# A graph network kernel: half-array products grouped behind the transposes of a block, bias and edge weights at 128 rows

## The chip, the cores and the metric

The kernel runs on one core of a Trainium2 chip. The metric is device microseconds of one execution, the median of several runs. One more execution was taken with the hardware profiler; its instructions are what the views below show. TensorE is called PE in them (PEld its weight load), VectorE DVE, ScalarE ACT, GpSimd POOL, SyncE SP; SPq is what SP issues to its DMA queue.

## The reference

50,000 nodes with 64 features, 50,000 edges sorted by destination. Four residual layers follow each other, each on `h = relu(layernorm(x))`:

```python
# 0: gated edges
m = sigmoid([h[dst], h[src], attr] @ W_f + b_f) * softplus(... @ W_s + b_s) * exp(-dist**2/18)
x = x + h + segment_sum(m, dst)
# 1: plain edges, one edge weight e
x = x + segment_sum(relu([h[src], h[dst], e] @ W1 + b1) @ W2 + b2, dst)
# 2: two attention layers (GATv2, 5 heads, self loops), softmax over dst, mean of heads, relu
x = x + g @ Wfc + bfc
# 3: graph convolution with degrees, batch norm, elu
x = x + layer3(h)
```

## The kernel before, in words

Edges and nodes are cut into 392 tiles of 128, four tiles a block, 98 blocks a stage (`blocks`, L724: six blocks, then a loop unrolled four times). Stages follow each other: setup, a node pass, `gated_edges` (PE 325 to 1055 us), a node pass, `plain_edges` (1243 to 1958), a node pass, `attention_logits` (2176 to 2910), softmax, messages, `attention_nodes` (3398 to 3650), the logits of the second attention layer (3708 to 4437), messages, `attention_nodes` again with the last layer (4925 to 5225), a node pass, `copied_edges`, the finish. Engines run their own instruction streams and meet at semaphores; the order of the work on each engine is written out by hand in its `body`.

Three of the stages gather rows of both ends of an edge with `NearRows`. SP loads for block n (L874 to L885) the edge positions `relb` (L877), four windows of node rows `near` (L882) and the rows that lie outside them, `rest` (L884), into `z`; it waits for `z_used` of block n-4 first. POOL gathers the source rows with four indirect DMAs (L870), also after `z_used` of block n-4. DVE makes the one-hot `hotT` (L894). PE then takes, in `turn` (L897), for two tiles at a time two fp32 transposes of `z` into the bank `zTp` (L905, full array) and eight matrix instructions, four products, of `near` with `hotT` (L909); the latter write 64 partitions each, two of them side by side on half of the array, and add to what the transposes wrote. The last one posts `z_used`. Another engine copies `zTp` to `zT`.

- `gated_edges`: PE does `turn(n)` with two transposes of the edge attributes (L1016), `scatter(n-2)` (L767), `project(n)`, which begins with a bf16 product of three ones rows and `bias3` (L1027; the bias is cut into three bf16 parts), followed by L1030 and L1034. ACT copies zT (L1057).
- `plain_edges`: PE does `turn(n)`, `second(n-1)` (L1219), `degrees(n-1)` (L1226), `scatter(n-2)`, `first_layer(n)`: a two-row fp32 product of the edge weights `aux` (L1239) and two half-array products (L1241). ACT copies zT (L1269), makes the one-hot of the scatter and the relu `uT` (L1274). SP stores the messages (L1189) five loads behind.
- `attention_logits`: PE does `turn(n)`, `project_whole(n-1)` (L1611, six groups of two fp32 products of 256 columns), `contract(n-2)` (L1594 to L1599, 32-column strips, posts `alp_ready`), `project_halves(n-1)` (L1618, 64-row tiles). DVE copies zT (L1681) and takes the logits (L1674); the copy of block n-1 comes behind the wait for `alp_ready` of block n-3.
- `attention_nodes`, second pass (g = 1): PE does two transposes (L2064), two more (L2080), `project` (L2073, 64-row tiles), and `last_layer`: a product of one row of ones and `bfc`, 256 columns in fp32 (L2086), then L2089. DVE multiplies (L2179), adds (L2184) and writes the new x (L2190); POOL adds (L2149 to L2158); ACT L2118, L2128.

In setup a chain of dependent DVE instructions prepares the weights; L485 to L492 cut the bias of `gated_edges` into three bf16 parts on three partitions, 128 columns wide.

## Time and profile before

| | us |
|---|---|
| median of three runs | 6153.05 |
| their range | 6148.98 to 6160.13 |
| profiled execution, first to last instruction | 6214.2 |

| engine | busy us | share |
|---|---|---|
| PE | 4419.2 | 71% |
| PE weight load | 3124.8 | 50% |
| DVE | 3312.8 | 53% |
| ACT | 3117.1 | 50% |
| POOL | 3300.7 | 53% |

The profiled execution has no time of its own beside its span; it is 1.0% above the median of the others. Busy shares are an average over some fifteen stages with different limits, so the slices of single stages have to be read. Matmuls overlap in the array and their ends are modelled: the distance from start to start tells the pace. A row of a stretch gives its start and end, its length, busy us and instructions of PE, PE weight load, DVE, ACT and POOL, then the granted TensorE clock, the busy share of the DMA engines and GB/s. An idle time in brackets behind an instruction is that of its engine just before it, with what ended it. The granted TensorE clock, 1.00 for 2.4 GHz, is a mean of 0.845 over the span.

### The profile page before, as it was taken

Reading aid. Unit: us, or ns where it says so; the run is one execution under the profiler, and the core shown is the slowest. Engines: PE = TensorE matmul, PEld = TensorE weight load, DVE = VectorE, ACT = ScalarE, POOL = GpSimd, SP = SyncE. Lnnn points to the kernel's source line nnn. Section 1 sums busy time; section 2 is a strip of 40 time slices with the busy share of each in tenths; the row PEclk is TensorE's granted clock in tenths of the full one; section 3 lists DMA queues with packets and bytes.
Section 4 is the critical chain, followed back from the end, with each engine's and each line's share of the span. In section 5 each row is a group of like instructions: output and inputs, shape, how many; then the busy total and the mean of one; then the engine's idle time right before and its main releaser. Section 6 shows DMA issues by size and latency. Waiting matters only on the chain. (4 is left out here: it accounts for less than half of the span.)

```text
span 6214.2 us, 127051 instructions
## 1 busy us (share of the span) xinstructions
PE 4419.2 (71%) x31655; PEld 3124.8 (50%) x31655; DVE 3312.8 (53%) x7235; ACT 3117.1 (50%) x8158; POOL 3300.7 (53%) x3372
## 2 busy tenths in 40 slices
PE   0078898089896089997498749999669896055564
PEld 0056676066664056665376326666447663054452
DVE  3833333766666432233787963333488788611156
ACT  0267776644555434444386214444358524644447
POOL 0855553155552165553586975555268687666620
PEclk6589998599998599999699979999879998576775
DMA  7545554655554744444133644444323333622224
GB/s 187 169 118 122 123 123 98 176 106 106 109 110 106 241 105 112 113 113 101 33 83 76 153 124 109 113 112 114 83 48 83 77 88 84 138 45 45 44 58 130
DMA packets 1393493, 665.08 MB, mean 107 GB/s; under 512 B 835537, under 2 KB 1341325, under 8 KB 1391594
## 3 DMA queue, kind: packets, MB, share of 16 engines
q1 hardware_dynamic: 1307980, 580.76, 37.4%
q0 software_dynamic: 64256, 65.93, 5.9%
q10 hardware_dynamic: 21124, 17.02, 0.9%
q8 instruction: 35, 0.57, 0.0%
q14 instruction: 98, 0.80, 0.0%
HBM read 393.69 MB, written 269.08 MB: 107 GB/s over the span
## 5 line engine op out<-in xcount | busy, mean ns | idle before, releaser
L870 POOL DMA_INDIRECT z_e<-h_d,src_i x784 | 756.8, 965 | 652.8 <-PE zTp_e L909 453.0
L1656 ACT ACTIVATE leak_l<-tp_l,bcat 128x512 f32<-128x512 f32 x588 | 365.9, 686 | 665.1 <-issue 422.4
L1681 DVE COPY zT_l<-zTp_l 128x512 f32<-128x512 f32 x196 | 135.5, 691 | 1005.7 <-DMA near_d<-gout_a 341.3
L754 ACT ACTIVATE hot_e<-iota_n,rel 128x256 f32<-128x256 f32 x1176 | 501.0, 502 | 322.9 <-DMA hn_a<-g_d 247.2
L784 DVE TENSOR_TENSOR acc<-acc,part_e 128x128 f32 x1176 | 336.8, 286 | 610.1 <-DMA hn_a<-g_d 247.4
L767 PE MATMUL part_e<-z_e,hot_e 128*128 128x128 f32 x1568 | 313.4, 376 | 436.7 <-DVE acc L784 226.9
L870 POOL DMA_INDIRECT z_l<-h_d,src_i x392 | 389.6, 994 | 326.4 <-PE zTp_l L909 229.2
L870 POOL DMA_INDIRECT z_l<-g_d,src_i x392 | 387.9, 989 | 324.9 <-PE zTp_l L909 230.0
L767 PEld LDWEIGHTS part_e<-z_e,hot_e 128*128 128x128 f32 x1568 | 285.2, 279 | 465.0 <-DVE acc L784 240.4
L905 PE MATMUL zTp_e<-ident,z_e 128*128 128x128 f32 x784 | 175.8, 306 | 480.4 <-DMA z_e<-rest_d 472.8
L1351 POOL DMA_INDIRECT z_e<-h_d,src_i x392 | 370.8, 946 | 222.7 <-issue 104.8
L767 PE MATMUL part_e<-m_e,hot_e 128*128 128x128 f32 x3136 | 408.5, 286 | 61.2 <-issue 28.1
L1661 ACT ACTIVATE leak_l<-tp_l,bcat 128x256 f32<-128x256 f32 x784 | 307.8, 475 | 283.1 <-PE tp_l L1618 252.2
L767 PEld LDWEIGHTS part_e<-m_e,hot_e 128*128 128x128 f32 x3136 | 392.5, 200 | 78.4 <-issue 39.9
L767 PEld LDWEIGHTS part_m<-m_m,hot_m 128*128 128x128 f32 x3136 | 365.9, 192 | 88.0 <-DVE acc L784 80.2
L767 PE MATMUL part_m<-m_m,hot_m 128*128 128x128 f32 x3136 | 403.2, 282 | 2.4 <-DVE acc L784 1.1
L1611 PE MATMUL tp_l<-zT_l,wcat 128*128 128x256 f32 x1176 | 376.2, 402 | 22.6 <-DVE zT_l L1681 14.1
L754 ACT ACTIVATE hot_m<-iota_n,rel 128x256 f32<-128x256 f32 x784 | 334.3, 497 | 110.0 <-PE part_m L767 108.5
L905 PEld LDWEIGHTS zTp_e<-ident,z_e 128*128 128x128 f32 x784 | 80.4, 143 | 566.5 <-issue 554.6
L905 PE MATMUL zTp_l<-ident,z_l 128*128 128x128 f32 x784 | 174.1, 304 | 264.8 <-DMA z_l<-rest_d 244.8
L1611 PE MATMUL tp_l<-zT_l,wswap_l 128*128 128x256 f32 x1176 | 355.6, 384 | 1.2 <-issue 1.2
L2179 DVE TENSOR_TENSOR prod_a<-xl_a,wself_a 128x640 f32<-128x640 f32 x392 | 303.9, 815 | 41.7 <-PE xl_a L2073 37.3
(362 smaller groups left out, 11787.7 us busy)
## 6 DMA issues: line engine op xcount, KB each, us to landing
near_e<-near_d SPq DMA_DIRECT2D x784, 64.0 KB
near_l<-near_d SPq DMA_DIRECT2D x784, 64.0 KB
h_d<-h SPq DMA_DIRECT2D x84, 448.0 KB
near_d<-h SPq DMA_DIRECT2D x84, 448.0 KB
m_d<-m_m SPq DMA_DIRECT2D x196, 138.0 KB
relb_e<-rel_d SPq DMA_DIRECT2D x196, 128.0 KB
z_e<-rest_d SPq DMA_DIRECT2D x196, 128.0 KB
relb_l<-rel_d SPq DMA_DIRECT2D x196, 128.0 KB
```

Source lines behind the costliest of these rows:

```text
L754: ins = self.nc.scalar.activation(self.hots[k][:, t, :], self.S["iota_n"][:, :], ACT.Abs, scale=-1.0, bias=self.S["rel"][:, ds(n * BLK + t ...
L767: mm = self.nc.tensor.matmul(self.parts[t // 2][:, t % 2, w, :], self.hots[k][:, t, w * P:(w + 1) * P], m[:, t, :], start=True, stop=True)
L784: ins = self.nc.vector.tensor_tensor(x, x, part[:, t % 2, :, 0:x.shape[2]], ALU.add)
L870: self.nc.gpsimd.indirect_dma_start(out=self.z[n % RINGS][:, t, SIDES[t % 2]], out_offset=None, in_=self.table[:, :], in_offset=bass.Indir ...
L905: self.nc.tensor.matmul(zTp[:, t * P:(t + 1) * P], self.z[k][:, t, :], ident[:, :], start=(t == 0), stop=False, is_transpose=True, skip_gr ...
L1351: nc.gpsimd.indirect_dma_start(out=z[k][:, t, 0:C], out_offset=None, in_=S["h_d"][:, :], in_offset=bass.IndirectOffsetOnAxis(ap=S["src_i"] ...
L1611: mm = nc.tensor.matmul(by_side(tp[q])[:, side], left[:, q, :], by_side(zT[k])[:, side], start=True, stop=True)
L1656: nc.scalar.activation(leak[u % 2][:, q, :], tp[q][:, :], ACT.Relu, bias=bcat[:, 0, q:q + 1], scale=1.0 - SLOPE).then_inc(leak_ready, 1)
L1661: nc.scalar.activation(by_side(leak[u % 2][:, 3 + q, :])[:, side], tp[3 + side][:, q * 2 * P:(q + 1) * 2 * P].rearrange("p (r e) -> p r e" ...
L1681: nc.vector.tensor_copy(zT[k][:, :], zTp[k][:, :]).then_inc(zT_ready, 1)
L2179: nc.vector.tensor_tensor(prod[k][:, 2 * q:2 * q + 2, :].rearrange("p t (h c) -> p t h c", h=H), xl[slot(u, q)][:, :, 0:HC].rearrange("p t ...
```

## The change

`turn` keeps its four transposes alone and no longer waits for `hotT`; the eight near products move to `spread`, which waits for `hotT`, goes over the windows outside and the tiles inside, and posts `z_used`. In `gated_edges` `spread(n)` stands behind the attribute transposes, in `attention_logits` behind `project_whole(n-1)`. In `plain_edges` the first layer is divided into `weights` (the edge weight product) and the rest, both a block later, as are the second layer, the degrees, the scatter and their helpers on ACT and DVE; the tail is a block longer. `aux`, `w1t`, `bias3` and `ones3` have 128 partitions of zeros beyond their rows; `bfc` is cut into three bf16 parts, `bfc3`, and the last layer adds it as one bf16 product with 128 rows.

```diff
--- before.py
+++ after.py
@@ -166,11 +166,12 @@
         w0 = sb("w0", [P, 2 * C])
         w0s = sb("w0s", [P, 2 * C])
         w0a = sb("w0a", [P, 2 * C])
-        bias3 = sb("bias3", [3, BLK * C], BF16)
-        ones3 = sb("ones3", [3, P], BF16)
+        bias3 = sb("bias3", [P, BLK * C], BF16)
+        bfc3 = sb("bfc3", [P, BLK * C], BF16)
+        ones3 = sb("ones3", [P, P], BF16)
         w1 = sb("w1", [P, C])
         w1s = sb("w1s", [P, C])
-        w1t = sb("w1t", [2, P])
+        w1t = sb("w1t", [P, P])
         b1 = sb("b1", [P, 1])
         w1b = sb("w1b", [P, P])
         b1b = sb("b1b", [P, C])
@@ -408,6 +409,8 @@
                 chain(nc.vector.memset(S["wfc"][:, :], 0.0))
                 chain(nc.vector.memset(S["w1b"][:, :], 0.0))
                 chain(nc.vector.memset(S["w1t"][:, :], 0.0))
+                chain(nc.vector.memset(S["bias3"][:, :], 0.0))
+                chain(nc.vector.memset(S["bfc3"][:, :], 0.0))
                 chain(nc.vector.memset(S["ones3"][:, :], 1.0))
                 nc.vector.memset(ones[:, :], 1.0).then_inc(s_blank, 1)
                 dve.wait_ge(s_loaded, 15 * 16)
@@ -489,7 +492,17 @@
                 for i in range(1, 3):
                     chain(nc.vector.scalar_tensor_tensor(out=whole[:, :], in0=cut[:, i, :], scalar=ident[0:3, i:i + 1], in1=whole[:, :],
                                                          op0=ALU.mult, op1=ALU.add))
-                chain(nc.vector.tensor_copy(S["bias3"][:, :].rearrange("p (q c) -> p q c", q=2), wide(whole[:, :], 1, 2)))
+                chain(nc.vector.tensor_copy(S["bias3"][0:3, :].rearrange("p (q c) -> p q c", q=2), wide(whole[:, :], 1, 2)))
+
+                for i in range(3):
+                    chain(nc.vector.tensor_copy(cut_b[:, 0:C], S["bfc"][0:3, :]))
+                    chain(nc.vector.tensor_copy(cut[:, i, 0:C], cut_b[:, 0:C]))
+                    chain(nc.vector.tensor_tensor(S["bfc"][0:3, :], S["bfc"][0:3, :], cut[:, i, 0:C], ALU.subtract))
+                chain(nc.vector.tensor_scalar(whole[:, 0:C], cut[:, 0, 0:C], ident[0:3, 0:1], None, ALU.mult))
+                for i in range(1, 3):
+                    chain(nc.vector.scalar_tensor_tensor(out=whole[:, 0:C], in0=cut[:, i, 0:C], scalar=ident[0:3, i:i + 1], in1=whole[:, 0:C],
+                                                         op0=ALU.mult, op1=ALU.add))
+                chain(nc.vector.tensor_copy(S["bfc3"][0:3, :].rearrange("p (q c) -> p q c", q=BLK), wide(whole[:, 0:C], 1, BLK)))
 
                 chain(nc.vector.tensor_reduce(bl_one[:, :], bl_col[:, :], AX.X, ALU.add))
                 chain(nc.vector.scalar_tensor_tensor(out=S["gcol"][:, :], in0=bl_one[:, :], scalar=1.0 / H, in1=S["gcol"][:, :],
@@ -899,15 +912,18 @@
         k, ident = u % RINGS, self.S["ident"]
         pe.wait_ge(gathered[k], 16 * BLK * (i + u // RINGS + 1))
         self.arrived(pe, u, i)
+        for t in range(BLK):
+            self.nc.tensor.matmul(zTp[:, t * P:(t + 1) * P], self.z[k][:, t, :], ident[:, :], start=(t == 0), stop=False, is_transpose=True, skip_group_check=True)
+
+    def spread(self, pe, n, u, zTp):
+
+        k = u % RINGS
         pe.wait_ge(self.hotT_ready, n + 1)
-        for r in range(0, BLK, 2):
-            for t in (r, r + 1):
-                self.nc.tensor.matmul(zTp[:, t * P:(t + 1) * P], self.z[k][:, t, :], ident[:, :], start=(t == 0), stop=False, is_transpose=True, skip_group_check=True)
-            for w in range(WIN):
-                for t in (r, r + 1):
-                    cols = slice(t * P, (t + 1) * P)
-                    mm = self.nc.tensor.matmul(zTp[SIDES[1 - t % 2], cols], self.near[k][:, t, w, :], self.hotT[u % 2][:, w, cols], start=False,
-                                               stop=(w == WIN - 1), skip_group_check=True)
+        for w in range(WIN):
+            for t in range(BLK):
+                cols = slice(t * P, (t + 1) * P)
+                mm = self.nc.tensor.matmul(zTp[SIDES[1 - t % 2], cols], self.near[k][:, t, w, :], self.hotT[u % 2][:, w, cols], start=False,
+                                           stop=(w == WIN - 1), skip_group_check=True)
         mm.then_inc(self.z_used, 1)
 
 
@@ -1015,6 +1031,7 @@
                     for q in range(2):
                         tr = nc.tensor.transpose(aTp[:, q * P:(q + 1) * P], att[k][:, 2 * q:2 * q + 2, :].rearrange("p t c -> p (t c)"), ident[:, :])
                     tr.then_inc(att_used, 1)
+                    near.spread(pe, n, u, zTp)
 
                 def project(n, u):
                     k = u % 2
@@ -1147,7 +1164,7 @@
         def ps(n, shape, count=2):
             return [ctx.enter_context(nc.psum_tensor(f"{n}_{name}_{k}", shape, F32)) for k in range(count)]
 
-        z, m, aux = ring("z", [P, BLK, 2 * C]), ring("m", [P, BLK, MOVED]), ring("aux", [2, 2, P])
+        z, m, aux = ring("z", [P, BLK, 2 * C]), ring("m", [P, BLK, MOVED]), ring("aux", [P, 2, P])
         zT, uT = ring("zT", [P, BLK * P], 2), ring("uT", [P, 2 * P], 2)
         zTp, uTp, mp, count = ps("zTp", [P, BLK * P]), ps("uTp", [P, 2 * P]), ps("mp", [P, BLK, C], 1)[0], ps("count", [P, TILES], 1)[0]
         sums = NodeSums(nc, S, ctx, name, WIDTH, S["deg_in"])
@@ -1175,13 +1192,13 @@
                     k = u % RINGS
                     near.load(sp, n, u)
                     need(sp, u_ready, n - RINGS + 1)
-                    sp.dma_start(aux[k][:, :, :], ew_rows[ds(n, 1)].rearrange("n r h e -> (n h) r e")).then_inc(aux_in[k], 32)
+                    sp.dma_start(aux[k][0:2, :, :], ew_rows[ds(n, 1)].rearrange("n r h e -> (n h) r e")).then_inc(aux_in[k], 32)
 
                 def load_last(n, u):
                     k, r0 = u % RINGS, n * BLK * P
                     near.load(sp, n, u)
                     sp.wait_ge(u_ready, n - RINGS + 1)
-                    sp.dma_start(aux[k][:, 0, :], io["edge_weight1"][r0:r0 + 2 * P, :].rearrange("(h e) a -> h (e a)", h=2)).then_inc(aux_in[k], 16)
+                    sp.dma_start(aux[k][0:2, 0, :], io["edge_weight1"][r0:r0 + 2 * P, :].rearrange("(h e) a -> h (e a)", h=2)).then_inc(aux_in[k], 16)
                     sp.dma_start(aux[k][0:1, 1, 0:LAST_E - 2 * P], ew[:, r0 + 2 * P:E]).then_inc(aux_in[k], 16)
 
                 def store(n, u):
@@ -1231,12 +1248,14 @@
                     pe.wait_ge(m_ready, n + 1)
                     sums.multiply(pe, n, u % 2, m[u % RINGS])
 
-                def first_layer(n, u, i):
+                def weights(n, u, r):
                     k = u % RINGS
-                    pe.wait_ge(aux_in[k], 32 * (i + u // RINGS + 1))
-                    pe.wait_ge(zT_ready, n + 1)
+                    pe.wait_ge(aux_in[k], 32 * (r + 1))
                     need(pe, uT_ready, n - 1)
                     nc.tensor.matmul(uTp[u % 2][:, :], S["w1t"][:, :], aux[k][:, :, :].rearrange("h r e -> h (r e)"), start=True, stop=False, skip_group_check=True)
+
+                def first_layer(n, u):
+                    pe.wait_ge(zT_ready, n + 1)
                     for half in range(2):
                         mm = nc.tensor.matmul(uTp[u % 2][half * C:(half + 1) * C, :], S[("w1", "w1s")[half]][:, :],
                                               zT[u % 2][:, :].rearrange("p (r h e) -> p h r e", h=2, e=P)[:, half],
@@ -1246,14 +1265,23 @@
                 def body(n, u, i):
                     turn(n, u, i)
                     if has(n, 1):
-                        second(n - 1, u + 1)
-                        degrees(n - 1, u + 1)
+                        weights(n - 1, u + UN - 1, i + (u - 1) // RINGS)
+                    near.spread(pe, n, u, zTp[u % 2])
+                    if has(n, 1):
+                        first_layer(n - 1, u + 1)
                     if has(n, 2):
-                        scatter(n - 2, u + UN - 2)
-                    first_layer(n, u, i)
+                        second(n - 2, u)
+                        degrees(n - 2, u)
+                    if has(n, 3):
+                        scatter(n - 3, u + UN - 3)
                 blocks(pe, body)
-                second(NB - 1, NB - 1)
-                degrees(NB - 1, NB - 1)
+                weights(NB - 1, NB - 1, (NB - 1) // RINGS)
+                first_layer(NB - 1, 1)
+                second(NB - 2, 0)
+                degrees(NB - 2, 0)
+                scatter(NB - 3, NB - 3)
+                second(NB - 1, 1)
+                degrees(NB - 1, 1)
                 for n in range(NB - 2, NB):
                     scatter(n, n)
                 pe.wait_ge(s_zero, 1)
@@ -1262,18 +1290,24 @@
 
             @block.scalar
             def _(act):
+                def hidden(n, k):
+                    act.wait_ge(u_ready, n + 1)
+                    need(act, mp_ready, n - 1)
+                    nc.scalar.activation(uT[k][:, :], uTp[k][:, :], ACT.Relu, bias=S["b1"][:, 0:1]).then_inc(uT_ready, 1)
+
                 def body(n, u, i):
                     k = u % 2
                     act.wait_ge(z_used, n + 1)
                     need(act, u_ready, n - 1)
                     nc.scalar.copy(zT[k][:, :], zTp[k][:, :]).then_inc(zT_ready, 1)
                     if has(n, 1):
-                        sums.hot(act, n - 1, 1 - k)
-                    act.wait_ge(u_ready, n + 1)
-                    need(act, mp_ready, n - 1)
-                    nc.scalar.activation(uT[k][:, :], uTp[k][:, :], ACT.Relu, bias=S["b1"][:, 0:1]).then_inc(uT_ready, 1)
+                        hidden(n - 1, 1 - k)
+                    if has(n, 2):
+                        sums.hot(act, n - 2, k)
                 blocks(act, body)
-                sums.hot(act, NB - 1, 1)
+                hidden(NB - 1, 1)
+                for n in range(NB - 2, NB):
+                    sums.hot(act, n, n % 2)
 
             @block.vector
             def _(dve):
@@ -1311,14 +1345,18 @@
 
                 def body(n, u, i):
                     near.hot(dve, n, u, i)
-                    los = sums.windows(dve, n - 3) if has(n, 3) else None
-                    digits(n, u)
-                    if has(n, 3):
-                        sums.add(dve, n - 3, los)
+                    los = sums.windows(dve, n - 4) if has(n, 4) else None
                     if has(n, 1):
-                        message(n - 1, u + UN - 1, i + (u - 1) // RINGS)
+                        digits(n - 1, u + 1)
+                    if has(n, 4):
+                        sums.add(dve, n - 4, los)
+                    if has(n, 2):
+                        message(n - 2, u + UN - 2, i + (u - 2) // RINGS)
                 blocks(dve, body)
-                message(NB - 1, NB - 1, (NB - 1) // RINGS)
+                digits(NB - 1, 1)
+                sums.add(dve, NB - 4, sums.windows(dve, NB - 4))
+                for n in range(NB - 2, NB):
+                    message(n, n, n // RINGS)
                 for n in range(NB - 3, NB):
                     sums.add(dve, n, sums.windows(dve, n))
 
@@ -1624,6 +1662,7 @@
                     turn(n, u, i)
                     if has(n, 1):
                         project_whole(n - 1, (u + 1) % 2)
+                    near.spread(pe, n, u, zTp[u % 2])
                     if has(n, 2):
                         contract(n - 2, u % 2)
                     if has(n, 1):
@@ -2083,7 +2122,7 @@
                 def last_layer(n, k):
                     pe.wait_ge(gT_ready, n + 1)
                     need(pe, x_done, n)
-                    nc.tensor.matmul(fcp[:, :, :], S["ones"][0:1, 0:P], wide(S["bfc"][0:1, :], 1, BLK), start=True, stop=False,
+                    nc.tensor.matmul(fcp[:, :, :].rearrange("p t c -> p (t c)"), S["ones3"][:, :], S["bfc3"][:, :], start=True, stop=False,
                                      skip_group_check=True)
                     for q in range(2):
                         mm = nc.tensor.matmul(fcp[:, 2 * q:2 * q + 2, :].rearrange("p t c -> p (t c)"), gT[k][:, q * P:(q + 1) * P], wfc[:, :],
```

## Rows read from the trace of the kernel before

**Rows 1.** Busy time per engine (instruction counts) in slices of gated, plain, logits, second attention_nodes.

```profile
400.00:600.00 200.00, 179.61 (x1510) 139.20 (x1509) 77.47 (x246) 161.97 (x441) 106.13 (x111) 0.96 0.52 122
1400.00:1600.00 200.00, 179.76 (x1360) 127.73 (x1358) 134.97 (x517) 101.12 (x192) 105.17 (x109) 0.95 0.51 107
2330.00:2485.00 155.00, 153.51 (x1224) 100.90 (x1227) 45.94 (x84) 71.70 (x147) 80.39 (x85) 1.00 0.47 112
4971.00:5126.00 155.00, 155.00 (x938) 98.33 (x936) 134.38 (x209) 38.96 (x104) 129.46 (x157) 1.00 0.34 88
```

**Rows 2.** Timeline of TensorE in plain_edges: start us, us, line, idle before and its releaser.

```profile
1509.38 0.43 PE L905 MATMUL zTp_e<-ident,z_e 128*128 128x128 f32 x2 [1.71 <-DMA z_e<-rest_d]
1509.75 0.66 PE L909 MATMUL zTp_e<-hotT_e,near_e 128*64 128x128 f32 x8
1510.34 0.44 PE L905 MATMUL zTp_e<-ident,z_e 128*128 128x128 f32 x2
...
1511.29 0.71 PE L1219 MATMUL mp_e<-w1b,uT_e 128*128 128x128 f32 x4
...
1514.38 0.69 PE L1239 MATMUL uTp_e<-aux_e,w1t 2*128 2x256 f32 x2
1515.00 0.43 PE L1241 MATMUL uTp_e<-zT_e,w 128*64 128x256 f32 x1
```

**Rows 3.** Timeline of SP's DMA queue in plain_edges.

```profile
1507.04 0.72 SPq L884 DMA_DIRECT2D z_e<-rest_d  x1
```

**Rows 4.** Waits in plain_edges, 1400 to 1800: us in total, times, longest us.

```profile
PE zTp_e L905 <- DMA z_e<-rest_d: 27.3, 19, 2.8
...
PE mp_e L1219 <- ACT uT_e L1274: 8.0, 18, 2.2
```

**Rows 5.** Waits in gated_edges, 500 to 900.

```profile
DVE hotT_e L894 <- DMA relb_e<-rel_d: 92.0, 30, 5.7
```

**Rows 6.** Instructions of single lines in plain_edges: count, min/median/max ns.

```profile
L905 PE MATMUL zTp_e<-ident,z_e x218: 272/324/477, 1405.0 to 1800.0; 128*128 128x128 f32 x109
...
L882 SPq DMA_DIRECT2D near_e<-near_d x219: 2/333/727, 1400.0 to 1796.5; - x110
```

**Rows 7.** Waits of SP's queue in the first logits stage, 2330 to 2796.

```profile
SPq L1560 <- DVE zT_l L1681: 3.6, 7, 0.6
```

**Rows 8.** Timeline of TensorE in the first logits stage.

```profile
2500.20 0.38 PE L1599 MATMUL alp_l<-leak_l,alate_l 128*32 128x256 f32 x1
...
2501.57 0.44 PE L905 MATMUL zTp_l<-ident,z_l 128*128 128x128 f32 x2
...
2504.24 0.59 PE L1611 MATMUL tp_l<-zT_l,wswap_l 128*128 128x256 f32 x2
...
2505.11 0.59 PE L1611 MATMUL tp_l<-zT_l,wswap_l 128*128 128x256 f32 x2
```

**Rows 9.** Timeline of VectorE in the first logits stage.

```profile
2502.87 0.69 DVE L1681 COPY zT_l<-zTp_l 128x512 f32<-128x512 f32 x1 [5.04 <-remote]
```

**Rows 10.** Timeline of the second attention_nodes pass, one block.

```profile
5031.99 1.35 PE L2073 MATMUL xl_a<-wl,hT_a 64*128 64x320 f32 x8
...
5032.97 1.55 DVE L2179 TENSOR_TENSOR prod_a<-xl_a,wself_a 128x640 f32<-128x640 f32 x2 [0.36 <-PE xl_a L2073]
...
5033.27 0.69 PE L2086 MATMUL fcp_a<-bfc,ones 1*128 1x256 f32 x2
...
5033.90 0.71 PE L2089 MATMUL fcp_a<-wfc,gT_a 128*128 128x128 f32 x4
...
5034.56 0.69 DVE L2184 TENSOR_TENSOR half_sum_a<-prod_a 128x512 f32<-128x512 f32 x1
...
5035.17 0.42 DVE L2190 TENSOR_TENSOR acc<-fcp_a,xo_a 128x256 f32 x1
```

**Rows 11.** Timeline of VectorE in setup.

```profile
127.89 0.21 DVE L485 CAST cut_b<-b 3x128 bf16<-3x128 f32 x1 [85.48 <-DMA bn<-in_L_gnn_beta_dram]
...
131.70 0.16 DVE L494 TENSOR_REDUCE bl_one<-bl_col 128x1 f32<-128x5 f32 x1
```

## The prediction

> **What bounds the kernel now.** I read the table of stage slices first [rows 1], because the whole-span average mixes stages with different limits. Each of the four edge stages the change touches (gated, plain, logits twice) and the two node passes of attention runs 98 blocks; four gathers on POOL belong to a block, so 200 us with 109 gathers in plain_edges are 27.25 blocks of 7.34 us, gated 7.2 us, logits 155/21.25 = 7.3 us. TensorE (PE) is 99% busy in logits and in the second attention_nodes pass, but only 90% in gated and plain: there about 0.7 us a block is left over, so PE is not what sets their pace.
>
> Next I read the timelines of PE and of SP's DMA queue in plain_edges. PE's block begins with the transposes L905, which waited 1.71 us for the rest rows [rows 2]; SP issued those at 1507.04 and took 0.72 us over it [rows 3], 1.6 us before PE began. The list of SP's own waits is empty in 400 us of either stage: it issues some nine transfers a block, one right behind the other. The waits of the stages say the same: in plain L905 for rest_d [rows 4], in gated hotT for relb, 92 us in 400 [rows 5], both loads from SP's queue. One near-row issue takes 0.33 us at the median and up to 0.73 [rows 6]: four of them a block, so a slow stretch costs SP a microsecond or two. So **SP's queue sets about 7.3 us a block in gated and plain**, whatever PE does. In logits both limits lie together: PE has no gap, and SP waited only 3.6 us in 466, for zT [rows 7], under 0.1 us a block.
>
> **The change, part by part.** The sum is made against the profiled execution's span, 6214.2 us; the median of the unprofiled runs, 6153.05, lies 1.0% below, and I carry the difference in us over to it.
>
> *Transposes together, then products.* Now a block is T2 N8 T2 N8 (matmul records; two near records run side by side). From the first L905 to L909 0.37, then 0.59 to the next L905 [rows 2]: twice 0.96, 1.92 us. A pair of transposes spans 0.43 where one lasts 0.32 [rows 2, 6], so one more costs 0.11; a near pair has the same 128 columns, so 0.11 too. The new order is 0.37 + 2 x 0.11 + 0.59 + 4 x 0.11 = 1.62. PE saves 0.3 us a block, of the two of four switches between full and half array that are gone.
>
> *Padded bias and edge weights.* L1239 with 2 rows takes 0.62 us up to L1241 for two passes of 256 columns [rows 2], where L1611 does four such passes in 0.87 (2504.24 to 2505.11, [rows 8]), 0.43 for two: about 0.2 saved, and perhaps 0.1 where it now stands between full-array work. With the 0.3 that is 0.6 us in plain. L1027 is one bf16 pass, half of that: 0.15, so 0.45 in gated. The copies, memsets and one-hots on ACT and DVE remain as many, only a block later.
>
> What that is worth: in **gated and plain nothing**, since the cover is SP's 7.3 us; PE just waits longer at L905. If that cover were gone, 0.45 x 98 = 44 and 0.6 x 98 = 59 us. Moved steps add no DMA; aux is now released one block later, but relb of block n is issued long after block n-4 was used (gathers of one block start every 7.3 us, four buffers), so the slack of about two blocks loses one. The message is one block later too, and SP stores it five loads behind.
>
> *Logits.* PE's own saving is the 0.3, plus one switch fewer before L1611, less a new one ahead of the near group: 0.3 to 0.4. SP's own work is about 7.2. So 7.3 falls to 7.2 and not to 6.9: I take 0.08 x 196 = **-15** (0 to -78).
>
> *attention_nodes, second pass.* Here PE has no gap and the period is 2.98 us: 938 matmul records in 155 us [rows 1], 18 a block. L2086 begins 5033.27 and L2089 5033.90 [rows 10]: 0.63 us, for two passes of 256 columns from one row and a switch. The new product is one bf16 pass at full array: between 0.12 (the pitch of a 128-column transpose, as a lower end) and 0.31 (half of L1239's 0.62, the upper). PE falls by 0.32 to 0.51, to 2.5 to 2.66. DVE is next: 1.55 + 0.69 + 0.42 = 2.66, with pipelining 2.62, and it sat idle 0.36 for L2073 [rows 10]. So the period goes to 2.62 to 2.66: 0.34 x 98 = **-33** (-31 to -35). That is the firm part.
>
> *Setup.* Thirteen more dependent DVE instructions; their thirteen twins ran 127.89 to 131.70 [rows 11], 3.8 us at 128 columns, these have 64: **+3** (0 to +4), on the path, since DVE's chain ends setup. The two memsets lie beside the loads of the weights; uncovered they would be under 1 us.
>
> *Tail of plain_edges.* One block's first layer, second layer, degrees and scatter more behind the last load: L1219 to L1239 is 3.1 and L1239 to the end of L1241 1.1 [rows 2], so 4.2 at most; part of it lies beside ACT's and DVE's work: **+3** (0 to +4).
>
> Sum: -15 - 33 + 3 + 3 = **-42**; profile 6172, median **6111**.
>
> **The rivals.**
>
> *PE's saving is realized.* SP's pace is not a constant: an issue takes 0.33 to 0.73 us [rows 6], and the unprofiled runs are 61 us shorter than the profiled one; if the long issues are partly the profile's own, the timed runs are closer to PE's pace in gated and plain. For: L1219 also waits for uT [rows 4], which the new order cures. Against: L905 waits for DMA in both stages. Full: -42 - 63 - 44 - 59 = -208, 5945; half of it, more likely, 6028. Chance 0.24.
>
> *A new wait in logits.* L1611 now stands right behind the transposes, and needs zT of the block before. DVE copies that (L1681) after L1599's signal: last L1599 at 2500.20 [rows 8], copy at 2502.87, 0.69 long [rows 9], so zT is there 3.4 us after it. Between the last L1599 and the new place of L1611 lie L1618 (1.37, to 2501.57) and four transposes (0.5): 1.87. PE would stall 1.5 us a block: 6.9 + 1.5 = 8.4 instead of 7.3, x 196 = +216, and with the other terms (-27) 6342. It decides once zT comes more than 1.87 + 0.4 after L1599, so when the copy starts over 1.6 us behind it. Against: the signal is late, as I read it, in the stretch in which issues take 0.7 us instead of 0.3 [rows 6]; that stretch goes with POOL's gather, which starts after the near products, and these come 2.6 us later in the new block (six L1611 groups of 0.43), away from L1599, and with a prompt signal the copy would be done at about 1.1. Chance 0.13. The Trainium skill ("TensorE: Matmul & The Clock Gate", "The cost: per-tile semaphore tail") gives a completion signal a tail of some tens of ns for one increment. By it L1611 never waits and the sum stays at -42. The 2.67 us between L1599 and L1681 don't agree with it, so the wait keeps its chance.
>
> *The bias buys nothing.* If the switch from L2073's 64-row tiles is what costs 0.6 us, the new product pays it too: -5 instead of -33 there, median 6139 to 6150. For: L2089 too follows L2086 only after 0.63, more than two passes take (0.43), so switches are part of the time. Chance 0.12.
>
> *The clock falls in logits*, now at 1.00 [rows 1], to the 0.96 of gated: 4% of 7.2 us is 0.3 a block, +57, median 6168. Chance 0.04. The Trainium skill (same page, "Part 4: PE-mode transpose") says that transposes do not count as TensorE being busy; four in a row would speak for this rival. The present pairs of transposes leave the clock at 1.00, so no run here shows it.
>
> **How the numbers follow.** My forecast 0.47 (6095 to 6130), the rivals 0.24, 0.13, 0.12, 0.04. Faster by more than 0.2% (12 us, about what a measurement of this kernel can tell) is the first two with a little of the third: 0.71; within 0.2%: 0.13; slower: 0.16. The range leaves out the new wait and the last part of PE's full gain: 6000 to 6165.
>
> **What would show it.** After the change: near records x16 in one group behind four transposes, 1.6 us; PE busy in gated and plain down to about 83%, with the gathers per 200 us unchanged (109) and L905 waiting longer for rest_d; logits 155 us slices with PE below 97% and 21.5 blocks; the second attention_nodes pass 2.62 to 2.66 us a block with DVE at 99%. More than 112 gathers in a 200 us slice of plain would prove the pace of SP wrong; idle PE before L1611 with DVE L1681 as releaser would be the new wait.

## The result: 2.1% slower, by a wait in attention_logits that depends on when TensorE's signals come

The change took 6281.02 us (median of 4, 6275.35 to 6288.80) beside 6154.98 us before (6148.98 to 6160.13): ratio 1.0207, 95% interval 1.0194 to 1.0219. The profiled execution spans 6277.4 us, 63 more than that of before. The timed difference is 126; before's profiled execution was 59 us longer than the median of its timed ones, the change's 4 us shorter. The slices of single stages after the change, in the columns of [rows 1]:

```profile
400.00:600.00 200.00, 169.74 (x1573) 146.68 (x1572) 80.03 (x252) 166.33 (x452) 108.98 (x113) 0.97 0.55 126
1400.00:1600.00 200.00, 165.88 (x1406) 132.56 (x1405) 141.00 (x538) 101.95 (x197) 112.82 (x115) 0.97 0.53 112
2330.00:2485.00 155.00, 135.43 (x1123) 93.45 (x1122) 41.07 (x76) 66.51 (x137) 72.79 (x76) 0.99 0.42 102
5050.00:5200.00 150.00, 135.35 (x891) 83.73 (x889) 134.09 (x210) 38.89 (x104) 129.69 (x158) 1.00 0.36 91
```

By POOL's counts gated takes 200/28.25 = 7.08 us a block (7.2 before), plain 6.96 (7.34), logits 155/19 = 8.16 (7.3), the second attention_nodes pass 2.85 (2.98). Such counts are coarse; the lengths of whole stages, from the first to the last matrix instruction, are firmer: gated -23 us, plain -13, the two logits stages +51 and +66, attention_nodes -11. PE, which had no gap in the logits slice of [rows 1], is 87% busy there. So the loss is in logits.

Part of these differences is not the change's. `g3_before_more_sp`, told below, has the old order in all stages and more work on SP in plain_edges alone; its before too took 6154 us, and its profiled execution (6274.8 us) lies near its timed ones (6278). Its slice of gated:

```profile
400.00:600.00 200.00, 186.31 (x1590) 143.96 (x1589) 80.60 (x253) 168.04 (x454) 109.91 (x114) 0.97 0.55 126
```

There gated takes 718.6 us from first to last matrix instruction, as in the change (718.5), where before's profiled execution had 741.4; the two logits stages take 745.2 and 745.9 (752.1 and 749.0 in before), copied_edges, which the change leaves alone, 555.6 (563.2; 555.7 in the change). So in these stages the profiled execution of before was some 40 us longer than another one of the old order, out of the 59. Against `g3_before_more_sp` the change gains nothing in gated and loses 58 and 69 us in logits.

One block of logits in the change, first PE, then DVE:

```profile
2501.96 0.38 PE L1637 MATMUL alp_l<-leak_l,alate_l 128*32 128x256 f32 x1
...
2503.34 0.66 PE L916 MATMUL zTp_l<-ident,z_l 128*128 128x128 f32 x4
2504.88 0.69 PE L1649 MATMUL tp_l<-zT_l,wcat 128*128 128x256 f32 x2 [0.89 <-issue]
...
2507.66 1.09 PE L925 MATMUL zTp_l<-hotT_l,near_l 128*64 128x128 f32 x16
```

```profile
2504.06 0.69 DVE L1720 COPY zT_l<-zTp_l 128x512 f32<-128x512 f32 x1 [5.71 <-issue]
```

L1637 is L1599 of [rows 8], L1649 is L1611, L1720 is L1681. The last product of contract stands at 2501.96; the copy of zT starts 2.10 us later and ends at 2504.75, and project_whole starts at 2504.88, 1.05 us later than its four transposes let it (it follows them after 0.49 us where nothing waits, in `r_after` below). That is the new wait of the second rival, place and all. The list of waits from 2330 to 2796 names DVE for only part of it:

```profile
PE tp_l L1649 <- issue: 33.5, 42, 1.0
PE tp_l L1649 <- DVE zT_l L1720: 17.0, 9, 2.3
```

The starts and ends in the trace settle the rest. In both logits stages together PE sat idle for 202 us ahead of project_whole, against 22 in the kernel before. In 167 of the 196 blocks this idle time was over 0.2 us, and each of these ended 0.05 to 0.15 us behind the end of a copy of zT; before had 12 such blocks. Where PE waited, the last relu of ACT that project_whole could also have waited for had ended 0.9 us or more earlier in nine blocks of ten.

### The profile page after: what moved, and what is told of

Read it like the earlier page. It is cut to its first block and busy times, and to the rows that moved or that the text cites. A ratio compares the mean times of both kernels' runs of the same rounds, so it can differ in the third digit from the quotient of the medians.

```text
span 6277.4 us, 126874 instructions
## 1 busy us (share of the span) xinstructions
PE 4214.5 (67%) x31557; PEld 3136.0 (50%) x31557; DVE 3308.4 (53%) x7250; ACT 3107.8 (50%) x8158; POOL 3294.4 (52%) x3372
## 5 line engine op out<-in xcount | busy, mean ns | idle before, releaser
L1720 DVE COPY zT_l<-zTp_l 128x512 f32<-128x512 f32 x196 | 135.5, 691 | 1130.9 <-issue 300.9
L1649 PE MATMUL tp_l<-zT_l,wcat 128*128 128x256 f32 x1176 | 384.1, 410 | 202.0 <-issue 108.2
L916 PE MATMUL zTp_e<-ident,z_e 128*128 128x128 f32 x784 | 129.7, 289 | 534.6 <-DMA z_e<-rest_d 522.4
L1649 PE MATMUL tp_l<-zT_l,wswap_l 128*128 128x256 f32 x1176 | 366.2, 394 | 0.0
L1649 PEld LDWEIGHTS tp_l<-zT_l,wcat 128*128 128x128 f32 x1176 | 217.1, 198 | 266.9 <-issue 196.8
L1994 DVE TENSOR_TENSOR prod_m<-xl_m,al 128x640 f32<-128x640 f32 x392 | 305.1, 820 | 37.2 <-PE xl_m L1955 14.2
```

What stands on the lines that cost most here:

```text
L916: self.nc.tensor.matmul(zTp[:, t * P:(t + 1) * P], self.z[k][:, t, :], ident[:, :], start=(t == 0), stop=False, is_transpose=True, skip_gr ...
L1649: mm = nc.tensor.matmul(by_side(tp[q])[:, side], left[:, q, :], by_side(zT[k])[:, side], start=True, stop=True)
L1720: nc.vector.tensor_copy(zT[k][:, :], zTp[k][:, :]).then_inc(zT_ready, 1)
L1994: nc.vector.tensor_tensor(heads[:, 2 * q:2 * q + 2], xl[slot(u, q)][:, :, 0:HC].rearrange("p t (h c) -> p t h c", h=H), wide(al[:, ds(n * ...
```

## A condition that none of the two profiles shows alone

The runs of the experiments met the kernel before at two paces: 5835 to 5840 us in five sets and 6154 in a sixth, as in the recorded result. One and the same chip number stands by a set of either pace, so it is a condition that comes and goes, and no fault of one chip (if the number always names the same one). Here are the near-row issues of SP in plain_edges, with the register move ahead of each; this stage is the same in both kernels. First before, as in [rows 6], then the kernel with the last layer's bias alone changed, at the quick pace:

```profile
L882 SPq MOVE near_e<-near_d x218: 3/29/721, 1400.4 to 1796.5; - x109
```

```profile
L895 SPq MOVE near_e<-near_d x258: 29/29/29, 1200.0 to 1597.7; - x129
```

Each of the 258 register moves takes 29 ns at the quick pace; at the slow pace the median is still 29, and the longest took 721. PE's signals follow: at the quick pace, with logits in the old order, DVE's copy starts 0.50 us behind contract's last product, where [rows 8, 9] had 2.67:

```profile
2202.90 0.38 PE L1631 MATMUL alp_l<-leak_l,alate_l 128*32 128x256 f32 x1
...
2206.19 0.70 PE L1643 MATMUL tp_l<-zT_l,wcat 128*128 128x256 f32 x2
```

```profile
2203.40 0.69 DVE L1713 COPY zT_l<-zTp_l 128x512 f32<-128x512 f32 x1 [4.83 <-issue]
```

All 196 blocks of both logits stages say the same. From contract's last product to the start of the copy the median is 2.50 us in before and 2.14 in the change, and 0.61 in `e2_last` and in `r_after`. The trace also records when a semaphore rises: contract's rises 0.04 us behind the end of its last product at the quick pace, at the median, and 1.98 (before) and 1.62 us (the change) behind it at the slow pace. DVE starts the copy 0.08 to 0.19 us behind that in most blocks at the slow pace. So it is the signal that is late, and not DVE.

The slices of `e2_last`, gated, plain, logits, second attention_nodes pass:

```profile
400.00:600.00 200.00, 200.00 (x1821) 158.64 (x1821) 92.58 (x294) 192.66 (x523) 128.57 (x131) 1.00 0.66 149
1200.00:1400.00 200.00, 200.00 (x1612) 144.19 (x1610) 158.28 (x614) 119.99 (x225) 126.25 (x130) 1.00 0.61 127
2050.00:2250.00 200.00, 200.00 (x1619) 132.08 (x1618) 59.88 (x112) 99.74 (x195) 104.49 (x112) 1.00 0.47 115
4700.00:4900.00 200.00, 181.66 (x1192) 112.09 (x1192) 180.70 (x281) 52.45 (x140) 174.10 (x211) 1.00 0.36 92
```

PE has no gap in gated, plain and logits: at this pace PE is the bound in these three, and SP is not. Every ratio below is against the kernel before, run in the same set.

## The experiments

**The parts one by one, and the whole again** (quick pace, before 5839.8 and 5836.8).

`e1_logits`: attention_logits alone in the new order.

```diff
                     if has(n, 1):
                         project_whole(n - 1, (u + 1) % 2)
+                    near.spread(pe, n, u, zTp[u % 2])
                     if has(n, 2):
                         contract(n - 2, u % 2)
```

> The kernel before with one part of the change alone: attention_logits takes the four transposes, project_whole of the block before, and then the eight near products; the other stages, the biases and the edge weights are as before. Theory A (PE waits for zT, whose copy DVE starts only 2 us after the last product of contract): the two logits stages take 50 to 66 us longer each in the profile, and this part alone makes the kernel 115 to 150 us slower than before, the whole of the change's loss and more. Rival B (the loss is spread over the stages, as with more wrong-clock time or slower queues everywhere): under 60 us of it appears here.

Measured 5751.25 us, 0.9845 (0.9832 to 0.9858): 89 us faster. Theory A fell, and there was no loss for rival B to spread: the signals were prompt.

`e2_last`: `bfc3`, its setup and L2086 as in the change, all else as before.

> The kernel before with the bias of the last layer as a bf16 product of 128 rows alone (setup's thirteen more DVE instructions included); all other stages keep their order and their two and three row products. Profile of the full change: the second attention_nodes pass is 11.5 us shorter, not the 33 I forecast. Theory A: the same here, 11 to 12 us less in that pass, 3 more in setup, -5 to -12 in all. Rival B (the pass was disturbed by the buffers or code around it): 25 to 33 us less.

Measured 5827.17, 0.9980 (0.9971 to 0.9989), -13, just past theory A's -12; the pass takes 287 us instead of 300.

`e3_plain`: plain_edges, `aux` and `w1t` as in the change.

> The kernel before with plain_edges alone as in the change (transposes and near products apart, first layer a block later, edge weights at 128 rows). Theory A, that SP's queue holds the pace there: within 10 us of before. Rival B, that PE's saving of 0.6 us a block comes through: up to 59 us less. The profile of the full change has this stage 13 us shorter.

Measured 5760.70, 0.9863 (0.9847 to 0.9878), -79, more than B's upper end.

`e4_gated`: gated_edges, `bias3` and `ones3` as in the change.

> The kernel before with gated_edges alone as in the change (transposes, attribute transposes, near products; bias at 128 rows). Theory A, SP's queue holds the pace: within 10 us of before. Rival B, PE's saving comes through: up to 44 us less. The profile of the full change has this stage 23 us shorter.

Measured 5817.20, 0.9962 (0.9949 to 0.9976), -23: more than theory A's 10, about half of rival B's 44. The slice of gated:

```profile
400.00:600.00 200.00, 189.15 (x1887) 166.57 (x1885) 96.48 (x305) 196.88 (x537) 131.92 (x135) 1.00 0.70 158
```

PE is at 95% now and ACT at 98% (96% in the old order). PE waits for ACT's one-hot in every block, here in `r_after`, whose gated stage is the same, from 500 to 900:

```profile
PE part_e L780 <- ACT hot_e L771: 21.3, 66, 0.5
```

So ACT takes over as the bound, and the rest of PE's saving is hidden. That is read from these rows; no run made ACT faster.

`r_after`: the whole change.

> The whole change again. The kernel before took 6155 us beside the change and 5840 us beside the last four kernels, where no completion signal of PE came late (0.3 to 0.42 us in each stage against 2.0 to 2.5) and no issue of SP took 0.7 us. Theory A: the change's worth depends on those signals. Where before takes about 5840, it takes 5840 - 88 - 79 - 22 - 13 = 5638 (parts add up, 5625 to 5655), and no instruction of PE waits for the zT copy; where before takes about 6155 it is again about 126 us slower. Rival B (the parts get in each other's way, a cause inside the change that the single parts don't have): slower than before also where before takes 5840.

Measured 5646.77 (5643.56 to 5649.25), 0.9674 (0.9661 to 0.9687): 190 us faster, where the parts add up to 203. Theory A in its first half; this set did not meet the slow pace. PE's idle time ahead of project_whole is over 0.2 us in 2 of 196 blocks, against 167 at the slow pace. So the same instructions are 3.3% faster at one pace and 2.1% slower at the other.

**Which wait turns late signals into a loss** (quick pace, before 5834.6). A dead addition puts the delay in by hand, in four kernels (the lines of the first two and the last):

```diff
                     need(dve, alp_ready, n - 1)
                     need(dve, hs_out[k], 32 * (UN // 2 * i + u // 2))
+                    if has(n, 2):
+                        nc.vector.tensor_tensor(idle[:, :, :], wide(still[:, :], 1, 12), wide(still[:, :], 1, 12), ALU.add)
                     nc.vector.tensor_copy(zT[k][:, :], zTp[k][:, :]).then_inc(zT_ready, 1)
```

`d1_before_late`: in the kernel before.

> The kernel before, with a dead addition of 1536 columns on DVE in both logits stages, between its wait for contract's signal and the copy of zT: about 1.6 us, so that the copy starts some 2.1 us after the last product of contract, as it did where the signals came late. Theory A (the old order leaves 3.3 us between that product and project_whole, the copy takes 0.7): within 20 us of before.

Measured 5851.24, 1.0026 (1.0015 to 1.0036): +17. The copy starts 2.28 us behind contract's last product at the median. The old order bears the delay.

`d2_after_late`: in the whole change.

> The same dead addition in the whole change. Theory A (the new order leaves 1.9 us only): project_whole waits about 1 us a block, logits rises from 6.9 to 7.8 us or more a block, 150 to 220 us more than the whole change without it, so at or a little above before minus the rest of the gains: ratio to before 0.99 to 1.005. Rival B (the copy's place is harmless, what made the change slower lies in other late signals): under 60 us more than the whole change.

Measured 5893.25, 1.0101 (1.0084 to 1.0118): 0.0427 above the change without it, 249 us, more than the 150 to 220 expected, and slower than before. PE and DVE in logits:

```profile
2200.12 0.38 PE L1638 MATMUL alp_l<-leak_l,alate_l 128*32 128x256 f32 x1
...
2201.49 0.66 PE L916 MATMUL zTp_l<-ident,z_l 128*128 128x128 f32 x4
2203.12 0.69 PE L1650 MATMUL tp_l<-zT_l,wcat 128*128 128x256 f32 x2 [0.97 <-DVE zT_l L1723]
```

```profile
2200.62 1.77 DVE L1722 TENSOR_TENSOR idle_l<-still_l 128x1536 bf16<-128x1536 f32 x1 [4.12 <-issue]
2202.31 0.68 DVE L1723 COPY zT_l<-zTp_l 128x512 f32<-128x512 f32 x1
```

The copy starts 2.19 us behind contract, as in the recorded trace (2.10), and project_whole stalls 0.97 us for it (0.89 there). The slice of 2050 to 2250 holds 102 gathers, 7.84 us a block, PE at 87%, the same share as in the recorded trace:

```profile
2050.00:2250.00 200.00, 174.05 (x1452) 120.05 (x1450) 95.34 (x126) 85.39 (x177) 109.55 (x102) 1.00 0.42 104
```

Rival C of the next expectation has ACT's relu in the copy's place, and the list of waits from 2050 to 2450 names it more often than the copy:

```profile
PE tp_l L1650 <- ACT leak_l L1701: 40.2, 38, 1.1
```

The trace speaks for the copy: in 187 of 196 blocks project_whole starts more than 0.2 us late, 205 us in all, and in eight of ten blocks it starts 0.134 to 0.147 us behind the copy's end, while the relu's end varies from 0.02 us to several us ahead of it. In many blocks here the relu ends late too, so this trace alone would not part the two; the next kernels do.

`e6_zT4` takes the copy out from behind contract: four zT buffers in place of two.

```diff
-        z, zT, logit = sb("z", [P, BLK, P], RINGS), sb("zT", [P, BLK * P]), sb("logit", [P, BLK * P])
+        z, zT, logit = sb("z", [P, BLK, P], RINGS), sb("zT", [P, BLK * P], RINGS), sb("logit", [P, BLK * P])
...
-                    need(dve, alp_ready, n - 1)
-                    need(dve, hs_out[k], 32 * (UN // 2 * i + u // 2))
+                    need(dve, alp_ready, n - 3)
+                    need(dve, hs_out[v], 32 * (i + u // RINGS))
```

> The change with four zT buffers in attention_logits in place of two, so that DVE copies zT of a block without waiting for contract of the block before the last; order of PE as in the change. Theory A (PE waits for that copy, the copy for contract's late signal): with late signals the two stages fall from 8.2 to 7.2 or 7.3 us a block, 150 to 190 us faster than the whole change; with prompt signals within 10 us of it. Rival C (PE waits for ACT's leak, whose signals are late too): under 50 us faster with late signals.

Measured 5624.59, 0.9639 (0.9626 to 0.9653), 22 us faster than the whole change, where at most 10 was expected.

`d3_zT4_late`: the addition in that kernel, where the copy now stands ahead of the wait for contract's signal and the addition behind it.

> The dead addition, behind the same wait, in the change with four zT buffers, where the copy does not stand behind contract's signal. Theory A: within 20 us of the four buffers without it (0.9639 of before). Rival B (DVE's load itself costs): as much more as in the whole change.

Measured 5641.88, 0.9671 (0.9655 to 0.9688), 19 us more than without it. DVE's load is not the cost; the copy's place behind the signal is.

`e5_spread_first`: in logits the near products right behind the transposes.

```diff
                     turn(n, u, i)
+                    near.spread(pe, n, u, zTp[u % 2])
                     if has(n, 1):
                         project_whole(n - 1, (u + 1) % 2)
-                    near.spread(pe, n, u, zTp[u % 2])
```

> The change with one edit: in attention_logits the near products stand right behind the four transposes, ahead of project_whole, so that project_whole comes 1.0 us later after contract, with as much done between as before. Theory A: with late signals about 150 us faster than the whole change and some 25 us faster than before; with prompt signals equal to the whole change within 20 us (the same products and about as many switches).

Measured 5677.54, 0.9729 (0.9716 to 0.9743): 31 us slower than the change, 11 more than allowed. In the change the transposes and project_whole, both on the full array, follow each other; here the near products part them, one switch more. The loss is 0.16 us a block; that it is the switch is argued, not shown.

`d4_first_late`: the addition in that kernel.

> The dead addition in the change with the near products right behind the transposes, where 3.0 us lie between contract's last product and project_whole. Theory A: within 30 us of that kernel without it (0.9729 of before), and so about 100 us or more faster than the whole change with the addition.

Measured 5707.89, 0.9781 (0.9765 to 0.9797): 30 us more than without it, 185 less than `d2_after_late`. With 3.0 us instead of 1.9 between contract and project_whole, the same delay is nearly free, but only just: at the median project_whole starts 0.13 us behind the copy's end, so a longer delay would cost.

`e7_first_zT4`: both edits.

> Both edits: near products right behind the transposes, and four zT buffers. With late signals: PE has no wait left in logits and shows whether SP's queue holds 7.2 us a block (theory A: within 15 us of the better of the two single edits) or PE's 6.9 comes through (up to 60 us faster). With prompt signals within 10 us of the near products first alone.

Measured 5658.63, 0.9699 (0.9685 to 0.9712), 19 us faster than the near products first alone, where at most 10 was expected, and 34 slower than `e6_zT4`. It did not meet the slow pace, so it tells nothing on SP's floor.

**SP's queue in plain_edges.** `g1_before_slow_sp` and `g2_plain_slow_sp` put `for _ in range(4): sums.windows(sp, n)` ahead of each load.

> The kernel before with four more reads of the block's four tile numbers on SP in each load of plain_edges (their values are not used): some 0.55 us each, so that SP's own work rises from 5.0 to about 7.2 us a block, as where issues took 0.7 us. Theory A (the pace is the larger of SP's and PE's): plain_edges rises from 6.3 to about 7.2 us a block, 80 to 100 us slower than before.

> The same four reads on SP, in the kernel with plain_edges alone as in the change. Theory A: the same 7.2 us a block, within 15 us of the kernel before with the reads, so the 79 us that the new order of plain_edges brought are gone, and it is 80 to 100 us slower than before. Rival B (the new order gains in itself, by taking waits away, also under a slow SP): still 50 us or more faster than the kernel before with the reads.

Measured 5837.64 (0.9998, 0.9988 to 1.0007) and 5759.89 (0.9867, 0.9851 to 0.9883), before 5838.5. The trace shows one tile-number read a block as ever: the compiler left the unused ones out. The two only repeat before and `e3_plain`, and tell nothing on SP.

`g3_before_more_sp` and `g4_plain_more_sp` issue real transfers:

```diff
+                def more(n):
+                    need(sp, spared, n * 64)
+                    for t in range(BLK):
+                        sp.dma_start(spare[0:16, t, :], S["near_d"][0:16, t, 0:C // 2]).then_inc(spared, 16)
```

> The kernel before with four more small transfers issued by SP in each load of plain_edges (16 rows of 128 bytes into a spare tile that nothing reads), about 0.5 us of SP's time each, in place of the reads of tile numbers, which the compiler had left out. SP's own work rises from 5.0 to about 7 us a block. Theory A (the pace is the larger of SP's and PE's): plain_edges goes from 6.3 to about 7 us a block, 60 to 80 us slower than before.

> The same four transfers in the kernel with plain_edges alone as in the change. Theory A: also about 7 us a block, within 15 us of the kernel before with the transfers: the gain of 79 us is hidden. Rival B (the new order gains in itself): 50 us or more faster than the kernel before with the transfers.

This set met the slow pace, before 6154.06. Measured 6278.07 (1.0198, 1.0181 to 1.0215), 124 us more than before where 60 to 80 were expected, and 6305.37 (1.0249, 1.0232 to 1.0267), 27 more again where 15 were allowed. The slices of plain_edges, old order and new, and the same stage of SP's queue in the old one:

```profile
1400.00:1600.00 200.00, 167.42 (x1196) 118.14 (x1196) 116.30 (x449) 88.51 (x167) 92.09 (x96) 0.89 0.41 96
```

```profile
1400.00:1600.00 200.00, 148.79 (x1170) 118.36 (x1167) 112.69 (x437) 84.31 (x163) 89.76 (x93) 0.90 0.40 93
```

```profile
1500.94 1.73 SPq L1178 DMA_DIRECT2D spare_e<-near_d  x4
1502.94 0.37 SPq L877 DMA_DIRECT2D relb_e<-rel_d  x1
1504.07 2.08 SPq L882 DMA_DIRECT2D near_e<-near_d  x4
1506.18 0.69 SPq L884 DMA_DIRECT2D z_e<-rest_d  x1
...
1509.17 1.73 SPq L1178 DMA_DIRECT2D spare_e<-near_d  x4
```

Four transfers more on SP take some 2.0 us of its time a block and make a block 1.27 us longer (124 us over 98 blocks), while PE goes to 84% busy, and in the new order to 74%. The list of SP's own waits from 1400 to 1800 is empty in before and in `g4_plain_more_sp` and has a single wait of 0.7 us in `g3_before_more_sp`. So at the slow pace SP's queue is on the path of plain_edges, as the forecast had it. It is not shown that it is the whole of it: the added time counts for some six tenths only, and the new order, with the same transfers on SP, does not tie but loses 27 us, for a reason that stays open. `e3_plain` without the transfers was not run at the slow pace, nor this pair at the quick one.

`e6b_zT4` and `e6c_zT4` sought the slow pace for the four zT buffers.

> The change with four zT buffers in logits a second time, for the case that the kernel before takes some 6155 us here, with late signals of PE. Theory A: there it is 60 us or more faster than before, where the whole change was 126 us slower; beside a before of 5840 it repeats 0.964.

> The change with four zT buffers once more, right after two runs that again met the slow condition (before at 6154 us). Theory A: if the condition still holds, logits keeps no stall at project_whole and takes 7.3 us a block or less in place of the change's 8.2, and the kernel is 30 us or more faster than before (6125 or less), where the whole change is 126 slower. Rival C (other late signals, of project_whole and project_halves to ACT, hold PE then): between 6125 and 6281. If the condition is gone: 0.964 of before again, which tells nothing new.

Measured 5625.87 (0.9637, 0.9621 to 0.9653) and 5624.62 (0.9636, 0.9623 to 0.9649), before 5838.5 and 5837.8: the quick pace both times. Whether the buffers cure the loss under real late signals was not seen; it is argued from the delay put in by hand. At the quick pace this kernel beats both, by 3.6% and by 22 us.

## Why the prediction was wrong

- **Logits, -15 forecast, about +117 in the trace.** This step of the prediction failed. The sum took it that nothing waits anew, and PE came to wait 202 us ahead of project_whole instead of 22; the wait stood among the rivals at 0.13, with 8.4 us a block and 6342 us, against 8.16 and 6281 measured. The argument against it was that the signal is late in the stretch of POOL's gather and would be prompt once the near products moved away. The trace after contradicts it for the most part: the copy starts over 1.6 us behind contract, the forecast's own threshold, in 140 of 193 blocks of the new order, against 182 in the old one, and the median falls only from 2.50 to 2.14 us. A delay that a trace shows in nearly every block ought to have been carried over to the new order as it stood. PE's own saving was a little more than the 0.3 to 0.4 forecast: 0.45 us a block at the quick pace (89 us over 196 blocks). It makes 88 us of gain, the wait 180 of loss: 92 of the 117; where the rest comes from was not found.
- **The Trainium skill's tail of some tens of ns for a signal** ("TensorE: Matmul & The Clock Gate", "The cost: per-tile semaphore tail"). The traces at the quick pace agree with it (contract's signal rises 0.04 us behind the product) and no wait appears; at the slow pace 1.6 to 2.0 us stand against it, and the measurement decides.
- **Gated and plain, nothing forecast.** At the slow pace the traces have -23 and -13 us, and the -23 is none of the change's, since the old order too took 718.6 us in `g3_before_more_sp`: the cover held, and the added transfers show that SP's queue is at least a part of it. The price if it were gone was 44 and 59; at the quick pace it is 23 and 79. Gated fell short because ACT, 98% busy, holds PE there, which the forecast did not name as next; plain went above 617 us for 98 blocks became 541, 0.78 us a block and not 0.6; which of its switches and waits the rest comes from was not taken apart.
- **attention_nodes, -33 forecast as the firm part, -11 measured.** L2086 sank as forecast: the new product (L2125 in the trace of the whole change at the quick pace) is followed by L2128 after 0.12 us. But the period is 2.85, not 2.62, because a wait took its place that the forecast left out:

```profile
4605.83 0.44 PE L2119 MATMUL turned_a<-ident,total_a 128*128 128x128 f32 x2 [0.54 <-POOL total_a L2197]
```

That row is of the whole change at the quick pace. PE's transposes of POOL's sum, three blocks back, now come before POOL has it, every second block: 26 times in 150 us, 14.7 us or 0.28 us a block, where the period lies 0.23 above 2.62. DVE, at 89%, is not the bound. No run took this wait away, so it is read from the rows alone.

- **Setup +3, tail +3.** Too small to be read from the timed runs.
- **The clock.** It stayed at 0.98 to 1.00 in logits at the slow pace and at 1.00 at the quick one, with four transposes in a row. The Trainium skill ("TensorE: Matmul & The Clock Gate", "Part 4: PE-mode transpose") says that transposes do not count as TensorE being busy; that cost nothing here.
- **The first rival**, PE's saving in full, gave 5945 from 6153, 208 us. Something like it happens at the quick pace (190), where PE is the bound: SP's pace is not a constant, as the rival said. But the long issues are not the profiler's, as it supposed, since profiled and timed executions agree at both paces to within 1%. And the 5945 and the 190 do not have the same parts: plain gave 79 instead of 59, gated 23 instead of 44, attention_nodes 13 instead of 33, so that they come near each other is in part luck.

## What to carry to other kernels

When work is moved, write down for each wait how long its signal takes in the trace at hand and how much work lies between producer and consumer in the new order; if the second is the smaller, the wait is the forecast and not a rival. An order with 1 us more between the two cost 31 us here and bore a delay put in by hand; buffers that take the consumer out from behind the signal bore it too and even gained 22. Neither was seen at the slow pace. And run the kernel before again with each set: a change may be worth 3% at one pace of the machine and cost 2% at the other.

## What was not expected of the hardware

The same kernel took 5840 us in some sets and 6154 in others. At the slow pace, in logits, DVE starts 2.1 to 2.5 us (medians) after TensorE's last product, 0.6 otherwise; the semaphore itself rises 1.6 to 2.0 us late, against 0.04. In plain_edges a register move on SP takes up to 721 ns, and 29 otherwise. The stages with gathers are the longer ones, copied_edges too (563 or 556 us against 479); the first messages stage and the second attention_nodes pass take the same time at both paces (340 and 300 us). What causes it is open.
